# Sums of x's blocks in a Strassen product: added by GpSimd's accumulating DMAs instead of VectorE

## The reference, cut to what matters

```
# x: (32, 64, 1024); i0, i2, i3: one index per batch
x = x + einsum('bct,bcd->bdt', x, W0[i0])      # 64 x 64 mixing of the channels of each batch
x = x + einsum('bct,bcd->bdt', x, W1[i0])      # the same with a second table
x = x + einsum('bsi,oi->bso', x, W)            # one 1024 x 1024 matrix for all batches
      + 0.5 * einsum('bsr,or->bso', einsum('bsi,bir->bsr', x, A[i2]), Bw)   # rank 32
x = x + einsum('bsi,boi->bso', x, W3[i3])      # one of 5 of 8 adapters, 1024 x 1024, per batch
```

## Time and profile before

| | |
|---|---|
| time, median of 3 runs | 383.15 us (382.86 to 383.18) |
| span of the profiled execution | 381.9 us, first to last instruction |
| own device time of the profiled execution | not given beside its span; the runs' median is 1.25 us above the span |
| TensorE busy | 375.4 us, 98% of the span |
| VectorE busy | 267.3 us, 70% |
| ScalarE busy | 224.6 us, 59% |
| GpSimd busy | 114.9 us, 30% |
| moved by DMA | 61.38 MB, 161 GB/s on the mean |

### The profile page before, as it was taken

One profiled execution on the slowest core, in us unless ns is written; L12 is line 12 of the kernel. 1 busy time (PEld: TensorE's weight loads), 2 busy tenths in 40 slices (PEclk: granted clock), 3 DMA queues, 4 the chain that ended last, 5 costly groups with the idle time before them and its releaser, 6 DMA issues.

```text
span 381.9 us, 7677 instructions
## 1 busy us (share of the span) xinstructions
PE 375.4 (98%) x1738; PEld 311.7 (82%) x1739; DVE 267.3 (70%) x302; ACT 224.6 (59%) x299; POOL 114.9 (30%) x156
## 2 busy tenths in 40 slices
PE   8999999999999999999999999999999999999995
PEld 5788888888888888888888888888888888888884
DVE  2796978856849888538869367854599635999653
ACT  3589568496246476235465465853677536779443
POOL 0000140100000000024765347563167532676600
PEclk9999999999999999999999999999999999999999
DMA  7985904640368484415437316652256622565223
GB/s 259 399 303 186 366 0 165 218 162 9 111 228 281 151 312 140 165 45 203 144 99 251 86 23 192 206 168 58 57 173 218 167 58 58 200 203 155 60 64 85
DMA packets 24187, 61.38 MB, mean 161 GB/s; under 512 B 1906, under 2 KB 2098, under 8 KB 24114
## 3 DMA queue, kind: packets, MB, share of 16 engines
q1 hardware_dynamic: 23648, 60.10, 47.6%
q10 hardware_dynamic: 466, 0.44, 0.4%
HBM read 52.15 MB, written 8.39 MB: 159 GB/s over the span
## 4 chain that ended last, share of the span: by engine, by line
PE 96%; DMA 2%; SPq 1%; DVE 0%; issue 0%; ACT 0%
PE ps L1526 45%; PE ps L1382 12%; PE ps L1383 12%; PE ps L1384 12%; PE ps L1409 4%; PE ps L1552 4%; PE ps L1618 2%; PE ps L1421 2%; DMA ring_f<-wt 2%; PE ps L1448 2%; PE ps L1567 0%; PE ps L1458 0%; SPq L315 0%; PE ps L1651 0%; DVE ring L906 0%; SPq L321 0%
## 5 line engine op out<-in xcount | busy, mean ns | idle before, releaser
L1526 PE MATMUL ps<-ring,aT 128*128 x752 | 173.2, 389 | 0.0
L1526 PEld LDWEIGHTS ps<-ring,aT 128*128 128x128 f32 x752 | 141.1, 188 | 29.6 <-issue 0.3
L1382 PE MATMUL ps<-ring 128*128 128x512 f32 x208 | 81.1, 390 | 0.0
L1383 PE MATMUL ps<-ring 128*128 128x512 f32 x208 | 81.0, 389 | 0.0
L1384 PE MATMUL ps<-ring 128*128 128x512 f32 x208 | 80.9, 389 | 0.0
L481 POOL TENSOR_TENSOR aT<-xT,aT 128x512 fp32r<-128x512 f32 (+1 forms) x36 | 56.2, 1581 | 47.4 <-ACT aT L766 42.4
L1273 DVE TENSOR_TENSOR ring<-raw,ring 128x1024 f32 (+1 forms) x40 | 61.7, 1600 | 6.2 <-ACT ring L752 6.2
L772 ACT ACTIVATE aT<-ps 64x1024 fp32r<-64x1024 f32 x32 | 32.7, 1023 | 47.5 <-PE ps L1526 47.1
L1301 DVE TENSOR_TENSOR stage<-ps,stage 64x1024 f32<-64x1024 f32 x30 | 36.7, 1222 | 28.9 <-ACT stage L781 28.2
L1290 DVE TENSOR_TENSOR aT<-ps,aT 64x1024 fp32r<-64x1024 f32 x32 | 39.1, 1222 | 21.5 <-ACT aT L772 20.8
L1382 PEld LDWEIGHTS ps<-ring 128*128 128x128 f32 x208 | 39.1, 188 | 8.1
(11 more groups left out here) (98 smaller groups left out, 326.9 us busy)
## 6 DMA issues: line engine op xcount, KB each, us to landing
raw<-w3t SPq DMA_DIRECT2D x40, 512.0 KB, 4.4
ring_f<-xt SPq DMA_DIRECT2D x8, 1024.0 KB, 8.7
raw<-xt SPq DMA_DIRECT2D x8, 1024.0 KB, 5.3
out<-stage SPq DMA_DIRECT2D x30, 256.0 KB, 3.2
ring_f<-wt SPq DMA_DIRECT2D x4, 1024.0 KB, 8.1
xT<-xt SPq DMA_DIRECT2D x3, 1024.0 KB, 10.4
xT<-wt SPq DMA_DIRECT2D x2, 1024.0 KB, 15.9
ring_f<-wt SPq DMA_DIRECT2D x4, 256.0 KB, 5.4
```

What stands on the lines that cost most here:

```text
L1382: pe.matmul(dst, hi_of(qw)[:, k, cs], hi_of(qx)[:, k, :], start=start and k == 0, stop=False, skip_group_check=True)
L1383: pe.matmul(dst, hi_of(qw)[:, k, cs], lo_of(qx)[:, k, :], start=False, stop=False, skip_group_check=True)
L1526: last = pe.matmul(acc(i)[:, n, :], x3_split(i, k, start, P), ring[:, bass.ds(off + (part * D + n * 512), 512)], start=(k == 0 and j == 0) ...
```

## The change

Five things change together.

1. The eight x sums (T3, T2, T4, T1, for j = 0 and 1) are no longer made by VectorE. GpSimd issues accumulating DMAs (`accum_op=ALU.add`) from x in HBM onto a block that SyncE has loaded before. Each block is added by two DMAs of 512 KB. T2 is now loaded block, plus a second, plus a third: two additions one behind the other.
2. T2 and T4 are both made in `stg`. T3 is made in `keep`. T1 is made in the raw place of operand 10, and in `kw`.
3. SyncE loads fewer blocks (the one-time buffer `b11`, operands 6 and 9 and two loads of `stg` go) and in another order. The first block for `keep` and the first for `stg` are loaded earlier.
4. Signs are turned: `s2()` subtracts where it added and has one instruction more, which subtracts twice the identity on the diagonal. `s4()` adds. The final `add_out` subtracts. These others keep their shape.
5. GpSimd's `w_eyes` now stand between its DMAs.

```diff
-    IN_STG = ("a", "B12_0", "B12_1", "B11_1", "B11_0 again", "B22_0", "B11_1 again", "B22_1")
-    in_stg = lambda name: 16 * (IN_STG.index(name) + 1)
+    two_of = lambda n: slice(HALF // 2 * n, HALF // 2 * (n + 1))
+    in_stg = lambda name: in_order(("a", "B11_0", "B11_1", "B22_0", "B22_1"), name)
+    in_keep = lambda name: in_order(("B12_0", "B12_1"), name)
+    in_kw = lambda name: in_order(("b", "A22", "B11_1"), name)
+    SUM = 32
...
             sp.dma_start(w2t, w_block(1, 1)).then_inc(s("w2t"), 16)
 
+            load_keep(2)
+            sp.wait_ge(s("a_tab"), 2)
+            load_stg(1, 0)
+            load_x(3, 2, 1)
             sp.wait_ge(s("b_split"), 4)
             load_kw(w_block(2, 2))
-            load_x(3, 2, 1)
-            load_keep(2)
-            sp.wait_ge(s("a_tab"), 2)
-            load_stg(1, 2)
-            sp.dma_start(b11, x_block(1, 0)).then_inc(s("b11"), 16)
             load_w(4, 2, 2)
-            load_x(6, 2, 0)
 
             sp.wait_ge(s("x_lo"), HALF * 6)
             load_keep(3)
-            sp.wait_ge(s("T4"), 1)
-            load_stg(1, 3)
-            sp.wait_ge(s("T3"), 2)
+            sp.wait_ge(s("x_lo"), HALF * 7)
             load_stg(1, 1)
-            load_x(9, 2, 1)
-            sp.wait_ge(s("T4"), 2)
-            load_stg(1, 0)
+            load_x(10, 1, 0)
             load_w(5, 1, 1)
-            load_x(10, 1, 2)
+            sp.wait_ge(s("x_lo"), HALF * 10)
+            load_stg(2, 2)
             load_x(11, 1, 2)
-            sp.wait_ge(s("T1"), 1)
-            load_stg(2, 2)
             load_w(6, 1, 2)
             sp.wait_ge(s("S4"), 1)
-            load_kw(x_block(1, 3))
+            load_kw(x_block(1, 1))
...
+            def plus(dst, half, c, name):
+
+                for n in range(2):
+                    pool.dma_start(dst[:, two_of(n), :], x_block(half, c)[:, two_of(n), :], accum_op=ALU.add)\
+                        .then_inc(s(name), 16)
+
+            def t3(j):
+                pool.wait_ge(s("keep"), in_keep(f"B12_{j}"))
+                plus(keep, 2, 2 + j, "T3")
+
+            def t2(j):
+                pool.wait_ge(s("stg"), in_stg(f"B11_{j}"))
+                plus(stg, 1, 2 + j, "T1")
+                pool.wait_ge(s("T1"), SUM * (j + 1))
+                plus(stg, 2, 2 + j, "T2")
+
+            def t4(j):
+                pool.wait_ge(s("x_lo"), HALF * (5 + 3 * j))
+                plus(stg, 2, j, "T4")
+
+            def t1_again():
+                pool.wait_ge(s("x_in10"), 16)
+                plus(raw_of(x_slot(10)), 1, 2, "T1_again")
+                pool.wait_ge(s("kw"), in_kw("B11_1"))
+                plus(kw, 1, 3, "T1_again")
+
+            t3(0)
+            t2(0)
             pool.wait_ge(s("S3"), 1)
             w_eyes(w2t, "S3")
+            t4(0)
             pool.wait_ge(s("w_in4"), 16)
             w_eyes(raw_of(w_slot(4)), "A22")
+            t3(1)
+            t2(1)
+            t4(1)
+            t1_again()
...
-            w_from(2, kw, "S2", 2)
-            x_from(4, stg, "T2", 1)
+            w_from(2, kw, "S2", 3)
+            x_from(4, stg, "T2", SUM)
...
-                dve.tensor_tensor(kw, kw, w1t, ALU.add).then_inc(s("S2"), 1)
+                dve.tensor_tensor(kw, w1t, kw, ALU.subtract).then_inc(s("S2"), 1)
                 dve.wait_ge(s("S2"), 1)
                 dve.tensor_tensor(kw, kw, w2t, ALU.subtract).then_inc(s("S2"), 1)
+                dve.wait_ge(s("S2"), 2)
+                v = raw[:, :, :].rearrange("p a n -> p (a n)")[:, 0:HALF * (D // 2 + P)]\
+                    .rearrange("p (k n) -> p k n", k=HALF)[:, :, 0:P]
+                dve.scalar_tensor_tensor(v, eye[:, 0:P].unsqueeze(1).to_broadcast([P, HALF, P]), -2.0, v, ALU.mult, ALU.add)\
+                   .then_inc(s("S2"), 1)
...
             s2()
             x_los(3)
             s3()
-            t3(0)
-            t2(0)
             low_parts(1)
```

More of the change, by code:

```diff
@@ L143, in build @@
     a_raw = raw[:, 2:4, :].rearrange("p a n -> p (a n)")[:, 0:NL * KT * R]
-    w1t, w2t, keep, b11 = out_block(2, 2), out_block(2, 3), out_block(1, 3), out_block(1, 2)
+    w1t, w2t, keep = out_block(2, 2), out_block(2, 3), out_block(1, 3)
     def unit(g, part):
@@ L202, in build @@
     w_before = lambda w: max(v for v in range(w) if w_slot(v) == w_slot(w))
-    IN_STG = ("a", "B12_0", "B12_1", "B11_1", "B11_0 again", "B22_0", "B11_1 again", "B22_1")
-    in_stg = lambda name: 16 * (IN_STG.index(name) + 1)
+    two_of = lambda n: slice(HALF // 2 * n, HALF // 2 * (n + 1))
+    in_order = lambda order, name: 16 * (order.index(name) + 1)
+    in_stg = lambda name: in_order(("a", "B11_0", "B11_1", "B22_0", "B22_1"), name)
+    in_keep = lambda name: in_order(("B12_0", "B12_1"), name)
+    in_kw = lambda name: in_order(("b", "A22", "B11_1"), name)
+    SUM = 32
+    block_of = lambda src, a, half: src[a:a + 1, 2 - half:3 - half].rearrange("a b k p n -> p (a b k) n")
+    x_block = lambda half, c: block_of(xt, c, half)
+    w_block = lambda out_half, in_half: block_of(wt, 2 - out_half, in_half)
     sem = {}
@@ L288, in _ @@
         def _(sp):
-            block_of = lambda src, a, half: src[a:a + 1, 2 - half:3 - half].rearrange("a b k p n -> p (a b k) n")
-            x_block = lambda half, c: block_of(xt, c, half)
-            w_block = lambda out_half, in_half: block_of(wt, 2 - out_half, in_half)
             def load_x(n, half, c):
@@ L310, in load_keep @@
             def load_keep(c):
-                sp.dma_start(keep, x_block(2, c)).then_inc(s("keep"), 16)
+                sp.dma_start(keep, x_block(1, c)).then_inc(s("keep"), 16)
             for k in range(HALF):
@@ L687, in _ @@
                 act.activation(mix_tab_of(rows, e), by_parity(ps_low[rows, :, :])[:, :, :, e, :], ACT.Copy).then_inc(s("mix_tab"), 1)
-            act.wait_ge(s("kw"), 16)
+            act.wait_ge(s("kw"), in_kw("b"))
             act.activation(b_split[:, :], b_raw, ACT.Copy, scale=0.5).then_inc(s("b_split"), 1)
@@ L707, in _ @@
             low_out(1)
-            w_from(2, kw, "S2", 2)
-            x_from(4, stg, "T2", 1)
+            w_from(2, kw, "S2", 3)
+            x_from(4, stg, "T2", SUM)
             c11(1, first_two)
             seed(0, last_two)
-            x_from(5, keep, "T3", 1)
+            x_from(5, keep, "T3", SUM)
             c11(1, last_two)
@@ L715, in _ @@
             u2(0)
-            x_from(6, None, "T4", 1)
+            x_from(6, stg, "T4", SUM)
             w_from(4, None, "A22", HALF)
@@ L722, in _ @@
             u3(0, last_two)
-            x_from(7, stg, "T2", 2)
+            x_from(7, stg, "T2", 2 * SUM)
             c21(0, first_two)
             seed(1, last_two)
-            x_from(8, keep, "T3", 2)
+            x_from(8, keep, "T3", 2 * SUM)
             c21(0, last_two)
@@ L730, in _ @@
             u2(1)
-            x_from(9, None, "T4", 2)
+            x_from(9, stg, "T4", 2 * SUM)
             u3(1)
             w_from(5, None, "S1", 2)
-            x_from(10, None, "T1", 1)
+            x_from(10, None, "T1_again", SUM)
             c21(1, first_two)
@@ L743, in _ @@
                 select(pair)
-            x_from(13, kw, "T1", 2)
+            x_from(13, kw, "T1_again", 2 * SUM)
             x_loaded(14)
@@ L924, in x_los @@
                     x_lo(n, src, ks)
[L926 to L958, removed]
             def s2():
@@ L963, in s2 @@
                 dve.wait_ge(s("w2t"), 16)
-                dve.wait_ge(s("kw"), 32)
-                dve.tensor_tensor(kw, kw, w1t, ALU.add).then_inc(s("S2"), 1)
+                dve.wait_ge(s("kw"), in_kw("A22"))
+                dve.tensor_tensor(kw, w1t, kw, ALU.subtract).then_inc(s("S2"), 1)
                 dve.wait_ge(s("S2"), 1)
                 dve.tensor_tensor(kw, kw, w2t, ALU.subtract).then_inc(s("S2"), 1)
+                dve.wait_ge(s("S2"), 2)
[3 more added lines that the diff above has]
+                   .then_inc(s("S2"), 1)
             def s3():
@@ L988, in s4 @@
                 v = raw_of(w_slot(6))
-                dve.tensor_tensor(v, v, kw, ALU.subtract).then_inc(s("S4"), 1)
+                dve.tensor_tensor(v, v, kw, ALU.add).then_inc(s("S4"), 1)
             def add_out(event, phase, j, src, dst, name, os=range(HALF)):
@@ L993, in add_out @@
                     wait_l2(dve, (event, j, o))
-                    dve.tensor_tensor(dst[:, o, :], ps_l2(phase, j, o), src[:, o, :], ALU.add).then_inc(s(name), 1)
+                    dve.tensor_tensor(dst[:, o, :], ps_l2(phase, j, o), src[:, o, :], ALU.subtract).then_inc(s(name), 1)
             c22 = lambda j: add_out("C22", 2, j, out_block(2, j + 2), out_block(2, j + 2), "c22")
@@ L1214, in _ @@
             w_los(1, raw_of(w_slot(1)))
-            dve.wait_ge(s("kw"), 16)
+            dve.wait_ge(s("kw"), in_kw("b"))
             dve.tensor_tensor(b_less, b_raw[:, cols_of(1)], b_raw[:, cols_of(2)], ALU.subtract).then_inc(s("b_less"), 1)
@@ L1239, in _ @@
             mix_twice()
-            t4(0)
-            x_los(6)
```

(8 more changed lines are left out.)

4 lines of the change are left out of this document (1 added, 3 removed).

## The result

The changed kernel takes 429.64 us (median of 4 runs, 427.02 to 430.52) against 383.11 us; the ratio is 1.1206, 95% interval 1.1171 to 1.1241. It is 46.5 us slower, where 13.3 us were forecast. The direction was right, the size was not.

The account below looks back on a forecast made before the run. TensorE was taken as the bound, busy 375.4 of 381.9 us without a gap behind 17 us. Terms 0 + 5.8 + 0 + 6.2 + 0 + 1.3 = 13.3 us gave 395.2, with 1.25 for the median 396.4; range 386 to 408.

Parts of the forecast that it names:

- c: kw's landing, in front of low_rank(1): kw comes late beside GpSimd's DMAs sharing the engines evenly; a wait of 5.8 us.
- e: T2 for j = 0: its second addition lands at 57.0, with 4 us of cover; nothing added.
- f: T2 for j = 1: serial load, two additions and split delay operand 7 at P6; a wait of 6.2 us.
- g: The rest, among it operands 9, 10, 13, keep, S4, outputs and w_eyes: all have time to spare; nothing added.
- h: TensorE's clock: one cold-start loss counted for two pauses, 1.3 us, bounds 0 and about 4.
- a: VectorE without the eight x sums: 18.3 us of busy time go, hidden under TensorE; worth 0.
- b: One instruction more in s2, in front of operand 3's low part: 0.69 us, so kw must land by 37.5.
- d: Price of one accumulated block of two DMAs: double data 5.3, 2.45 around it, two issues of 0.37; 8.5 us.
- A: Time of one accumulated block (two DMAs of 512 KB), from GpSimd's wait to the landing; taken as 8.5 us.
- dear rival: Accumulated blocks cost 11 to 13 us, DMAs hardly overlapping or GpSimd slow to build them; time 407, chance 0.21.

Follow-up runs that it names:

- e9: e6 with two swaps in VectorE's order: operand 3's low part before S2, operand 15's before the outputs C12 of j = 0; 383.84 us, ratio 1.0014.
- e5: e3 with GpSimd's first DMA made to wait until the block in kw has landed; 398.49 us, ratio 1.0403.
- e2: The changed kernel with GpSimd's DMAs plain, overwriting instead of adding (the sums of x's blocks left out); 393.11 us, one run.
- e1: The changed kernel with the scratch for GpSimd's DMA descriptors doubled from 1024 to 2048 bytes of a partition; 410.63 us, ratio 1.0701.
- e8: The changed kernel with 1280 instead of 1024 bytes of scratch for GpSimd's DMAs and nothing else; 407.55 us, ratio 1.0624.
- e3: The changed kernel with T2 made by VectorE in one addition (loaded block plus T3) for both j; 401.53 us, ratio 1.0477.
- e10: e8 with T2 for j = 1 put before T3 for j = 1 on GpSimd's queue; 404.15 us, ratio 1.053.
- e6: e5 with 1280 instead of 1024 bytes of scratch for GpSimd's DMAs; 389.26 us, ratio 1.0172.
- e7: The changed kernel with each block added by four DMAs of 256 KB instead of two of 512 KB, scratch still 1024; 427.74 us, ratio 1.1152.
- e4: The changed kernel with 125 matmuls on constants put in front of P6 for j = 1 to keep TensorE busy; 428.37 us.

## Why the prediction was wrong

| step | forecast us | measured us |
|---|---|---|
| c, low_rank(1) | 5.8 | 4.5 |
| e, P6 for j = 0 | 0 | 6.6 |
| f, P6 for j = 1 | 6.2 | 16.8 |
| g, operands 10 and 13 to 15 | 0 | 4.1 + 1.9 + 2.5 |
| h, the clock | 1.3 | 11.5 |

**What bounds the kernel, and a and b: right.** TensorE was the chain, VectorE's work was worth nothing (e9 shows it with the rest repaired), and the instruction more takes 0.69 us.

**c: right in kind and nearly in size.** kw landed 4.1 us later instead of 6.4. e5 parts the wait: 2.6 us from GpSimd's traffic, 1.8 without it, most of this from SyncE's early loads and the longer S2. The even sharing of the engines was a little too dear.

**d is the step that failed.** "two issues of 0.37" took it that the second DMA of a block follows at once. The double data was right (200 GB/s): GpSimd's queue moved 10.49 MB with and without adding, but its packets took 14.9% of the 16 engines' 428.5 us in the changed kernel and 7.7% of 391.3 us in e2, about twice the engine time. The reason given for it, that the destination is read too, no run shows by itself. The second half waits for a place in the scratch: 11.7 us for 8.5. With place for it the block costs 8.7 to 8.8 (e1, e8), close to the number of the forecast, though not by its terms: one issue takes 1.2 us and not 0.37, but the second runs while the first one's data move, and these move more slowly than counted at the start (95.28 to 104.02 in e1, of it about 6.2 with data moving where 5.3 were counted). That nearness is in part luck. I had named A = 12 as the dear rival, with chance 0.21 and a time of 407; the rival's cause in part ("the two DMAs of a block hardly overlap") is what happened, and its sum of 407 was still 22 us short: 3.9 in e, 3.6 in f, 8.5 in g and 8.9 in h, less 1.3 in c and 1.2 at the start.

**e: mis-sized through d.** Six DMAs of about 6 us one behind the other, the first 9.6 because it shared with kw, put T2's landing at about 70.7 instead of 57.0 (ScalarE starts on it at 70.79). e3, e1 and e8 have no wait there.

**f: both inputs off.** Of the 10.6 us over the forecast, 6.4 are 2 x (11.7 - 8.5). Another 3.6 come from the start of T2: stg's load was issued at 91.13 and T2 began at 99.85, 8.7 us later instead of 5.1. The load itself was in time in the changed kernel:

```profile
raw<-xt SPq DMA_DIRECT2D x1, 1024.0 KB, 5.2
```

It landed at 96.3. T2 was kept by T3 for j = 1, which stands in front of it on GpSimd's queue and has no place in the forecast's sum: T3's second half, issued at 94.02, held the one place until 99.85. With two places (e8) T3 moved its data beside stg's load instead and made that load late. e10 takes T3 out of the way, and the wait falls from 12.4 to 7.3.

**g: called safe without a price for contention.** T1 for operand 10 ran beside four of SyncE's loads, its first half took 9.5 us (145.32 to 154.78) instead of 5.8, and TensorE waited 4.1. The whole block took 18.6 us (163.89, when ScalarE starts on it). In e6 and e8, with the faster block, that wait is gone.

**h: counted once, happened behind five of six waits.** From 125 to 131 us, behind the 16.8 us, the changed kernel's table by stretches gives a clock of 0.50:

```profile
109.00:125.00 16.00, 0.00 (x0) 0.00 (x0) 0.71 (x1) 1.86 (x2) 2.44 (x2) 0.57 0.52 86
125.00:131.00 6.00, 5.33 (x13) 4.22 (x14) 4.40 (x7) 5.01 (x9) 1.21 (x1) 0.50 0.31 53
```

The waits of 4.5, 6.6, 4.1 and 2.5 us had a stretch at 0.50 behind them too. The one of 1.9 us at P5 for j = 1 had none:

```profile
198.00:200.00 2.00, 2.00 (x10) 1.61 (x10) 2.00 (x3) 2.00 (x3) 0.00 (x0) 1.00 0.08 20
```

Five such stretches in 11.5 us make 2.3 each, where the forecast had one of 1.3, read from the start of the kernel (named there for the clock, begin only at 17 us). From 1 to 4 us, under those first matmuls, the table by stretches of the kernel before gives 1.00, so that they were slow from a low clock is shown by no run. Nor does any run show a border at about 6 us of pause: 1.8 us in e5 had a slow stretch behind it, 3.7 us in e3 had none. In three of the profiles, waits came with a slow clock as follows: e6 3.7 and 2.4 us, e3 13.1 and 6.3, changed 36.3 and 11.5. In e6 the wait of 2.2 us had the slow stretch behind it and the one of 1.5 us had none, so a wait of 2.2 us cost about as much again.

## What to carry to other kernels

Work that nobody waits for is worth nothing when it is taken away, and putting it elsewhere can only add a wait: look for a gap of the bounding engine first. A price for a pair of transfers needs the answer whether the two overlap; where the trace does not show it, take both ends into the range, and carry the dear end through every step that uses it, not only one. When one queue serves all such transfers in order, work out when each may start behind the one before, and price the plain loads beside it too.

## What the runs showed of the hardware

- An accumulating DMA from GpSimd moves its data at about 200 GB/s (changed kernel) where a plain load has 390.
- How many of GpSimd's DMAs are under way is set by the scratch: with 1024 bytes one accumulating DMA of 512 KB (changed kernel), with 1280 two (e8), with 2048 three (e1). 256 bytes were worth 22 us here (e8).
- In e7 a fourth DMA found a place only about 1 us after the data of all three before it had moved.
- A plain load of 1 MB by SyncE landed 9.6 us after its issue with two of GpSimd's accumulating DMAs moving beside it (e8), and 5.2 us after it without them (e10).
- GpSimd spends 1.2 us on the issue of an accumulating DMA of 512 KB (changed kernel) and 0.73 on a plain one (e2); SyncE spent 0.37 on that of kw's load of 1 MB.
- TensorE's clock fell to 0.50 behind a pause of only 1.9 us in e4 and one of 1.8 us in e5, and stayed at 1.00 behind one of 1.9 us in the changed kernel, one of 1.5 us in e6 and one of 3.7 us in e3. The length of a short pause alone does not say which.
